# A decoder layer on one core: values, keys and queries of the prologue, and six small pieces of work in the stages, at other places

## The chip, the cores and the metric

The kernel runs on one core of one Trainium2 chip. The metric is the time of one execution on the device in microseconds (us), as the median of several executions. The core's engines are TensorE (PE, matrix multiplication), VectorE (DVE), ScalarE (ACT), GpSimd (POOL) and SyncE (SP); each runs its own instructions strictly in order, and semaphores order them among each other. SP issues most transfers, ACT a few.

## What is computed

Four batches of 512 tokens with 256 features pass through three sublayers, each followed by x + sublayer(x) and a layer norm: gated linear attention, cross attention to a context, and a feed-forward part with a token shift. Shortened:

```python
def _gla_scan(q, k, v, log_gate):            # 16 heads, DK = 8, DV = 16
    def step(state, inp):
        qq, kk, vv, gg = inp
        state = state * gg[..., None] + kk[..., :, None] * vv[..., None, :]
        return state, jnp.einsum('bhd,bhde->bhe', qq, state)
o = _gla_scan(q, k, v, log_sigmoid(x @ Wg1 @ Wg2) / 16)
o = (o - mean(o)) * rsqrt(var(o) + EPS)       # within a head
x = layernorm(x + silu(x @ Wg + bg) * o @ Wo)

Q, K, V = x @ W_q, ctx @ W_k, ctx @ W_v       # 16 heads of 16
attn = softmax(einsum('bqhd,bkhd->bhqk', Q, K) / 4)
x = layernorm(x + einsum('bhqk,bkhd->bqhd', attn, V) @ W_o + b_o)

xr, xk = mu_r * x + (1 - mu_r) * x_prev, mu_k * x + (1 - mu_k) * x_prev
x = layernorm(x + sigmoid(xr @ W_r.T) * (square(relu(xk @ W_k.T)) @ W_v.T))
```

## The kernel before

**Stages.** After a prologue come six stages (`STEPS`). In stage s batch s+2 (called r) is projected and scanned, batch s+1 (o) ends the gated attention and makes keys and queries, batch s (b) runs the cross attention, batch s-1 (f) the feed-forward part and batch s-2 (e) its last norm. A stage is 16 rows n of 4 quarters i; at each (n, i) every engine's code does one score tile of b and whatever tables and `if at == ...` lines put there. So the order of work on every engine is written by hand. A score tile `s{n}.{i}` is a matmul of keys and queries on PE into bank 5 or 6 (L718), then an exponential on ACT (L1230); a row of four tiles is followed by the product with the values on PE (`value_row`, L732). The exponential needs the row maximum of the head: a matmul of queries and keys (L709, L853 in the prologue) and a maximum on DVE (L1652), then `max_parts`, a transpose on PE and a small transfer (`max_rows`) into three extra rows of QS. `Q` and `K` are split in three bfloat16 parts (hi, mid, lo): ACT and DVE take turns on the bank (`first_part`, `rest_of`, `second_part`, `last_part`), SP writes the parts to memory (`part_out`) and reads them back by groups of four heads into KS and QS (`keys_of`, `queries_of`).

**Scans.** The gated attention is 16 scans on DVE (L1797 in the prologue, L1556 later). Each needs a product with the keys on POOL (L2029, L1971), and is followed by a product with the queries on POOL (L1982). Four such products are summed on PE (`reduce_four`, L689), four times a batch; `SUM_QUARTERS` gives the quarters.

**Prologue.** It does the gated attention of batch 0, most of that of batch 1 (`EARLY_SCANS` scans ahead of the first maxima, the rest behind them), the keys and queries of batch 0, the first 16 maxima (heads 0 to 3) and the values of batch 0 (`first_values`, L842: eight matmuls, one behind each of the first eight maxima). `keep_busy` (L957) runs bfloat16 matmuls whose result nobody reads; they only keep PE occupied. `PROLOGUE` lists which bank each matrix uses, in order. SP's queue in the prologue is written out: all K parts of half 0, a transfer of tokens, all K parts of half 1, keys of groups 0 and 1, Q parts, queries of groups 0 and 1.

**Other pieces that the change touches.** `heads_together` issues four small transfers which bring a group's normalised context into the layout of the output projection (`OD`); they wait for `normal`. `invert` is ACT's inverse of the softmax denominators (two instructions, L1260, L1262), which waits for DVE's `spread` (L1672); `normalise` is the product behind it. `group_ends` gives both their quarters. `norm(1, ...)` applies the second layer norm in four DVE instructions (L1542), the `Relu` of the feed-forward part is one ACT instruction for each half (L1201).

## Time and profile before

| | |
|---|---|
| median of 3 executions | 496.71 us (496.16 to 502.71) |
| the profiled execution | 498.83 us, of which 496.5 us are the span that the trace covers |
| busy over the span | PE 438.0 us, DVE 380.2, ACT 286.9, POOL 227.6 |

By stage, from the trace by stretches (a stage is taken from its first score tile):

| stretch | length | PE | DVE | ACT | POOL | granted clock |
|---|---|---|---|---|---|---|
| prologue 0:94.6 | 94.6 | 85.3 | 77.2 | 35.1 | 66.0 | 0.98 |
| stage 0 94.6:190.8 | 96.2 | 84.6 | 74.8 | 59.2 | 59.4 | 0.96 |
| stage 1 190.8:298.2 | 107.4 | 97.9 | 86.9 | 71.9 | 64.4 | 1.00 |
| stage 2 298.2:384 | 85.8 | 78.5 | 70.3 | 57.0 | 29.1 | 1.00 |
| stage 3 384:463 | 79.0 | 67.4 | 52.6 | 49.6 | 8.7 | 0.98 |
| tail 463:496.5 | 33.5 | 24.4 | 18.4 | 14.1 | 0.0 | 0.96 |

How to read it: the rows below are of the timeline unless said otherwise. A row is start, duration, engine, line, what is written from what, the number of instructions; in brackets the idle time of the engine before it and what ended that.
### The profile page before, as it was taken

The numbers are of one execution on the slowest core, as the hardware profiler recorded it, in microseconds if no ns is written. First come the engines' busy times: TensorE is split into PE (matmuls) and PEld (weight loads), VectorE is DVE, ScalarE is ACT, GpSimd is POOL, SyncE is SP. The second block draws the span as 40 slices with busy tenths as digits, with TensorE's granted clock in tenths as the row PEclk, the third lists the DMA queues.
The fourth block names the chain that finished last, engine by engine and source line by source line (L and its number), as shares of the span: only waits on it lengthen the run. The fifth ranks groups of instructions, "written<-read, shape, count | busy, mean of one in ns | idle before, by whom it ended". The sixth has DMA issues, their size and how long they took to land.

```text
span 496.5 us, 6244 instructions
## 1 busy us (share of the span) xinstructions
PE 438.0 (88%) x1919; PEld 185.7 (37%) x1919; DVE 380.2 (77%) x638; ACT 286.9 (58%) x513; POOL 227.6 (46%) x226
## 2 busy tenths in 40 slices
PE   8999888988988899899889888997999888888994
PEld 3433434233432214254343323443433332333563
DVE  4889897967668898577897898599858579754285
ACT  4244362354476666654777866646786545687443
POOL 5568798442158995531489785525022011020000
PEclk9999998999989989999999999999999989999998
DMA  6746565232297521324955304230243310000101
GB/s 202 269 130 178 140 179 133 64 90 73 86 239 184 140 67 46 84 64 120 236 143 131 74 2 116 69 82 2 65 107 75 76 53 3 2 0 1 44 1 44
DMA packets 26512, 47.33 MB, mean 95 GB/s; under 512 B 5456, under 2 KB 16368, under 8 KB 26480
## 3 DMA queue, kind: packets, MB, share of 16 engines
q1 hardware_dynamic: 24512, 44.05, 33.5%
q10 hardware_dynamic: 1968, 2.88, 2.2%
q8 instruction: 16, 0.26, 0.2%
q14 instruction: 16, 0.13, 0.1%
HBM read 35.19 MB, written 9.96 MB: 91 GB/s over the span
## 4 chain that ended last, share of the span: by engine, by line
PE 52%; DVE 27%; ACT 7%; issue 5%; POOL 4%; DMA 2%; SPq 1%; ACTq 1%; DVEq 0%; POOLq 0%
PE bank L657 16%; DVE MX L1652 12%; PE bank L671 9%; PE bank L732 7%; PE bank L718 5%; PE bank L709 5%; DVE W L1556 4%; PE bank L822 3%; ACT PT L1230 3%; POOL W L1982 2%; PE bank L689 2%; DVE st L1529 1%; DMA xT<-in_xT 1%; PE bank L948 1%; DVE den L1672 1%
## 5 line engine op out<-in xcount | busy, mean ns | idle before, releaser
L1652 DVE TENSOR_REDUCE MX<-bank 128x1 f32<-128x512 f32 x256 | 166.1, 680 | 71.6 <-PE bank L709 67.5
L1230 ACT ACTIVATE PT<-bank 128x512 f32<-128x512 f32 x256 | 144.9, 597 | 86.6 <-PE bank L718 81.6
L709 PE MATMUL bank<-KS,QS 96*128 96x512 bf16 x240 | 88.4, 386 | 21.9 <-DVE MX L1652 21.2
L718 PE MATMUL bank<-QS,KS 99*128 99x512 bf16 x256 | 95.9, 388 | 11.2 <-ACT PT L1230 8.5
L732 PE MATMUL bank<-PT,Vs 128*32 128x512 f32 x512 | 70.8, 625 | 4.5 <-ACT PT L1230 4.3
L1982 POOL TENSOR_TENSOR W<-qT,W 128x512 f32<-128x512 f32 x48 | 63.2, 1320 | 20.6 <-DVE W L1556 9.0
L718 PEld LDWEIGHTS bank<-QS,KS 99*128 99x128 bf16 x256 | 24.2, 98 | 101.1 <-issue 58.1
L709 PEld LDWEIGHTS bank<-KS,QS 96*128 96x128 bf16 x240 | 23.4, 98 | 68.9 <-DVE MX L1652 45.2
L1971 POOL TENSOR_TENSOR W<-kT,W 128x512 f32<-128x512 f32 x32 | 41.6, 1299 | 6.7 <-ACT kT L1080 6.7
L1556 DVE TENSOR_TENSOR_SCAN W<-bank,W 128x512 f32<-128x512 f32 x32 | 38.7, 1210 | 0.2 <-ACT bank L1095 0.2
L1797 DVE TENSOR_TENSOR_SCAN W<-bank,W 128x512 f32<-128x512 f32 x32 | 38.1, 1210 | 0.4 <-DVE oS L1816 0.2
L2016 POOL TENSOR_TENSOR MP<-MX,zero 128x16 bf16<-128x16 f32 x15 | 3.6, 241 | 57.4 <-DVE MX L1652 28.9
L1982 POOL TENSOR_TENSOR W<-xr,W 128x512 f32<-128x512 f32 x16 | 21.2, 1332 | 11.4 <-DVE W L1797 11.4
L1949 POOL TENSOR_TENSOR rs<-mv,eps 128x4 f32<-128x4 f32 x9 | 1.8, 202 | 49.5 <-DVE mv L1535 49.5
L732 PEld LDWEIGHTS bank<-PT,Vs 128*32 128x32 f32 x512 | 10.3, 109 | 28.1 <-issue 24.1
L1955 POOL TENSOR_TENSOR OT<-OT,den 128x512 f32<-128x512 f32 x9 | 12.2, 1360 | 17.7 <-ACT den L1262 17.7
L2029 POOL TENSOR_TENSOR W<-xr,W 128x512 f32<-128x512 f32 x16 | 20.2, 1274 | 0.1
L689 PE MATMUL bank<-W,hsel 128*32 128x512 f32 x128 | 17.0, 605 | 2.9 <-POOL W L1982 2.9
L1962 POOL TENSOR_TENSOR ka<-ka 128x512 f32<-128x512 f32 x4 | 4.2, 1040 | 30.8 <-ACT ka L1201 30.8
L957 PE MATMUL bank<-identb 128*128 128x512 bf16 x71 | 17.8, 379 | 0.0
L671 PE MATMUL bank<-wo,oS 128*128 128x256 f32 x64 | 15.1, 380 | 1.8 <-DVE oS L1821 1.8
L657 PE MATMUL bank<-x1T,xwq 128*128 128x512 f32 x32 | 15.0, 596 | 0.9 <-ACT x1T L1330 0.8
(228 smaller groups left out, 721.9 us busy)
## 6 DMA issues: line engine op xcount, KB each, us to landing
W<-v_rows SPq DMA_DIRECT2D x20, 512.0 KB, 8.9
k_parts<-parts SPq DMA_DIRECT2D x24, 128.0 KB, 2.3
KS<-k_parts SPq DMA_DIRECT2D x16, 192.0 KB, 3.5
q_parts<-parts SPq DMA_DIRECT2D x24, 128.0 KB, 2.4
QS<-q_parts SPq DMA_DIRECT2D x16, 192.0 KB, 3.5
cT<-in_cT SPq DMA_DIRECT2D x4, 512.0 KB, 4.3
xtok<-in_x SPq DMA_DIRECT2D x4, 512.0 KB, 10.0
W<-v_rows ACTq DMA_DIRECT2D x4, 512.0 KB, 5.9
```

Of the source, the lines that this page charges most:

```text
L657: ins = pe.matmul(out, w_of(k), x_of(k), start=(k == 0), stop=(k == ND - 1))
L671: ins = pe.matmul(bank(name, b)[:, half * D:(half + 1) * D], x[:, k, tt * P:(tt + 1) * P], w[:, k, :], start=(k == 0), stop=(k == tiles - 1))
L689: ins = pe.matmul(bank(f"o{g}", a)[32 * j:32 * j + 32, :], hsel[:, i, :], W[:, 4 * q + j, :], start=(i == 0), stop=(i == 1))
L709: pe.matmul(bank(n, b)[:, :], QS[0:NS, h, i * P:(i + 1) * P], KS[0:NS, h, :], start=True, stop=True).then_inc(filled(n, b), 1)
L718: pe.matmul(bank(name, b)[:, :], KS[0:NR, h, kt * P:(kt + 1) * P], QS[0:NR, h, :], start=True, stop=True).then_inc(filled(name, b), 1)
L732: ins = pe.matmul(bank(f"pv{g}")[32 * j:32 * j + 32, :], Vs[:, kt, 4 * g + j, :], PT[:, n % 2, j, :], start=(kt == 0), stop=(kt == NT - 1))
L1230: act.activation(PT[:, n % 2, j, :], bank(name, b)[:, :], ACT.Exp).then_inc(emptied(name, b), 1)
L1556: dve.tensor_tensor_scan(W[:, e, :], bank("decay", r)[:, :], W[:, e, :], 0.0, ALU.mult, ALU.add).then_inc(s_done, 1)
L1652: dve.tensor_reduce(MX[:, NT * h + i:NT * h + i + 1], bank(n, b)[:, :], AX.X, ALU.max).then_inc(emptied(n, b), 1)
L1797: dve.tensor_tensor_scan(W[:, e, :], bank("decay", r)[:, :], W[:, e, :], 0.0, ALU.mult, ALU.add).then_inc(s_done, 1)
L1971: pool.tensor_tensor(W[:, e, :], kT[:, :], W[:, e, :], ALU.mult).then_inc(u_pool, 1)
L1982: pool.tensor_tensor(W[:, e, :], qT1 if r == 1 else qT[:, :], W[:, e, :], ALU.mult).then_inc(p_done, 1)
```

## The change

In the prologue:
- PE: the eight value matmuls leave the maxima. Four stand behind K1 (bank 4), where 12 fillers become 5; four behind the first sum of batch 1 (bank 1), where 8 fillers become 6. One filler stands behind each of the first eight maxima instead.
- DVE: scan 1 of batch 1 moves from ahead of the norm (`scale_half`) to behind the first rest of K; the third part of K1 moves ahead of scan 5; scan 7 ahead of the rest of Q0; `EARLY_SCANS` is 12, so scan 12 moves behind the maxima. The bfloat16 copy of the identity moves to ACT.
- SP: keys of group 0 are read as soon as K's half 0 is out, the last two parts of half 1 follow, and the keys of group 1 come behind the queries of group 0. The tokens of batch 1 are loaded at the end.
- ACT: the copy of the batch 1 queries (`qT1`) moves behind the sigmoids, the squares and the decay; each half of the values is copied when it is there.

In the stages:
- the second sum at quarter 49 for 48, the first half's copy (`oS`) at (13, 0) for (12, 2); the last sum of batch 1 one quarter later, with its copy at (1, 1) for (1, 0);
- `heads_together(b, 2)` leaves the end of the stage and stands ahead of that of group 3 in the next stage, behind keys, queries and context;
- in stage 3 the inverse of group 3 at (1, 1) for (1, 0) and its product at (1, 2) for (1, 1);
- the second norm in two halves, at (4, 1) and (4, 2);
- in stage 3 both Relu on DVE instead of ACT.

```diff
-SUM_QUARTERS = {(40, 48, 57, 66)[q]: q for q in range(RQ)}
+SUM_QUARTERS = {(40, 49, 57, 66)[q]: q for q in range(RQ)}
-EARLY_SCANS = 13
+EARLY_SCANS = 12
+FIRST_BUT_ONE = ((0, 1), (0, 2))
-    ends = [(1, f, NG - 1, FIRST_THING)] if f is not None else []
+    ends = [(1, f, NG - 1, FIRST_BUT_ONE if f == LAST - 1 else FIRST_THING)] if f is not None else []
...
 # SP, a stage
+                    heads_together(f, 2)
                     heads_together(f, 3)
...
-                if b is not None and b < LAST:
-                    heads_together(b, 2)
...
 # PE
-                late = NT * (H + at[0]) + at[1] - (o == 1)
+                late = NT * (H + at[0]) + at[1] - 2 * (o == 1)
...
                 by_feature("K1", 0, xwk, 1, cT)
-                keep_busy("gt0", 0, 12)
+                for n in range(NT):
+                    first_values(n)
+                keep_busy("gt0", 0, 5)
...
                 reduce_four(1, 0)
-                keep_busy("s0.0", 0, 8)
+                for n in range(NT, 2 * NT):
+                    first_values(n)
+                keep_busy("s0.0", 0, 6)
                 for h in range(4):
                     for i in range(NT):
                         first_max(h, i)
-                        if h < 2:
-                            first_values(NT * h + i)
-                        else:
-                            keep_busy("s0.0", 0, 1)
+                        keep_busy("s0.0", 0, 1)
...
 # ACT
-                if at == (12, 2):
+                if at == (13, 0):
                     act.wait_ge(r_done, count(RQ, r, RQ // 2))
...
-                if at == (1, 0):
+                if at == ((1, 1) if o == 1 else (1, 0)):
                     act.wait_ge(r_done, count(RQ, o, RQ))
...
-                if at in ((9, 1), (10, 1)):
+                if at in ((9, 1), (10, 1)) and f < LAST - 1:
...
 # DVE
-                if at == (4, 1):
+                if at in ((4, 1), (4, 2)):
                     dve.wait_ge(*full_of("t1", f - 1))
                     dve.wait_ge(x3_done, count(NT, f, 0))
-                    norm(1, xb, x2, x2_done, f)
+                    norm(1, xb, x2, x2_done, f, ((0, 1), (2, 3))[at[1] - 1])
...
+                if at in ((9, 1), (10, 1)) and f == LAST - 1:
+                    m = at[0] - 9
+                    z = bank(f"f{m}")[:, :]
+                    dve.wait_ge(*full_of(f"f{m}", f))
+                    dve.wait_ge(*full_of("w1", f - 1))
+                    dve.scalar_tensor_tensor(ka[:, m, :], z, 0.0, zero[:, 0:1].broadcast_to([P, S]), ALU.max, ALU.max).then_inc(emptied(f"f{m}"), 1)
```

**DVE in the prologue, from the gate of batch 0 to the parts of the queries.** `oS` is the output of the gated attention, `W` the scans, `xtok` the residual, `parts` the bfloat16 parts. Before:

```order
L1816 TENSOR_TENSOR oS<-bank,kz 128x512
L1797 SCALAR_TENSOR_TENSOR W<-bank,W 128x512
L1821 TENSOR_TENSOR oS<-bank,oS 128x512 x2
L1510 SCALAR_TENSOR_TENSOR bank<-bank,parts 128x512
L1797 SCALAR_TENSOR_TENSOR W<-bank,W 128x512
L1826 TENSOR_TENSOR xtok<-bank,xtok 128x512
L1529 BN_STATS st<-xtok 128x6 x2
L1826 TENSOR_TENSOR xtok<-bank,xtok 128x512
L1529 BN_STATS st<-xtok 128x6 x2
L1535 BN_AGGR mv<-st 128x2 x4
L1514 TENSOR_TENSOR parts<-bank,parts 128x512
```

Of the change:

```order
L1827 TENSOR_TENSOR oS<-bank,kz 128x512
L1832 TENSOR_TENSOR oS<-bank,oS 128x512 x2
L1517 SCALAR_TENSOR_TENSOR bank<-bank,parts 128x512
L1808 SCALAR_TENSOR_TENSOR W<-bank,W 128x512 x2
L1837 TENSOR_TENSOR xtok<-bank,xtok 128x512
L1536 BN_STATS st<-xtok 128x6 x2
L1837 TENSOR_TENSOR xtok<-bank,xtok 128x512
L1536 BN_STATS st<-xtok 128x6 x2
L1542 BN_AGGR mv<-st 128x2 x4
L1521 TENSOR_TENSOR parts<-bank,parts 128x512
```

The scan between the two products that write `oS` is gone, so the norm (the pair that writes `oS` from a bank and itself) stands directly behind the gate, and two scans stand ahead of the residual.

**SP's queue in the prologue, from the K parts to the queries.** `KS` and `QS` are the keys and queries that PE reads. Before:

```order
L475 DMA k_parts<-parts 16x8x512 x3
L550 DMA xtok<-in_x 128x4x256
L475 DMA k_parts<-parts 16x8x512 x3
L464 DMA KS<-k_parts 48x1x2048
L464 DMA KS<-k_parts 32x1x2048
L464 DMA KS<-k_parts 16x2048
L464 DMA KS<-k_parts 48x1x2048
L464 DMA KS<-k_parts 32x1x2048
L464 DMA KS<-k_parts 16x2048
L475 DMA q_parts<-parts 16x8x512 x3
L469 DMA QS<-q_parts 48x1x2048
```

Of the change:

```order
L475 DMA k_parts<-parts 16x8x512 x4
L464 DMA KS<-k_parts 48x1x2048
L464 DMA KS<-k_parts 32x1x2048
L464 DMA KS<-k_parts 16x2048
L475 DMA k_parts<-parts 16x8x512 x2
L475 DMA q_parts<-parts 16x8x512 x3
L469 DMA QS<-q_parts 48x1x2048
L469 DMA QS<-q_parts 32x1x2048
L469 DMA QS<-q_parts 16x2048
```

The tokens and the second set of keys no longer stand ahead of the Q parts; four K parts instead of six are ahead of the first keys.

**PE in the prologue, from K1 to the first maxima.** Before:

```order
L657 MATMUL bank<-cT,xwk 128x512 x2
L957 MATMUL bank<-identb 128x512 x12
L679 MATMUL bank<-ident,x1b 128x128 x8
L657 MATMUL bank<-x1T,xwq 128x512 x4
L657 MATMUL bank<-ka,wg 128x512 x4
L689 MATMUL bank<-W,hsel 32x512 x4
L957 MATMUL bank<-identb 128x512 x8
L853 MATMUL bank<-KS,QS 128x512
L842 MATMUL bank<-xwv,cT 128x256
L853 MATMUL bank<-KS,QS 128x512
```

Of the change:

```order
L658 MATMUL bank<-cT,xwk 128x512 x2
L843 MATMUL bank<-xwv,cT 128x256 x4
L959 MATMUL bank<-identb 128x512 x5
L680 MATMUL bank<-ident,x1b 128x128 x8
L658 MATMUL bank<-x1T,xwq 128x512 x4
L658 MATMUL bank<-ka,wg 128x512 x4
L690 MATMUL bank<-W,hsel 32x512 x4
L843 MATMUL bank<-xwv,cT 128x256 x4
L959 MATMUL bank<-identb 128x512 x6
L854 MATMUL bank<-KS,QS 128x512
L959 MATMUL bank<-identb 128x512
```

The value matmuls (`xwv,cT`) stand ahead of the transposes and ahead of the maxima; between the maxima stand fillers.

## Rows read from the trace of the kernel before

**Rows 1.** PE's waits, 94:497: engine, line, releaser, total us, times, longest.
```profile
PE bank L709 <- DVE MX L1652: 21.2, 36, 1.5
...
PE bank L718 <- DMA cT<-in_cT: 1.5, 1, 1.5
```

**Rows 2.** Timeline: start, us, engine, line, out<-in, count, idle before; gate and norm.
```profile
47.26 1.08 ACT L1365 ACTIVATE bank<-bank 128x512 f32<-128x512 f32 x2
...
53.08 1.26 DVE L1821 TENSOR_TENSOR oS<-bank,oS 128x512 f32<-128x512 f32 x2
...
54.40 3.72 PE L671 MATMUL bank<-wo,oS 128*128 128x256 f32 x16 [1.79 <-DVE oS L1821]
```

**Rows 3.** Timeline, 59 to 69 us: statistics to the query projection.
```profile
59.67 0.38 DVE L1535 BATCH_NORM_AGGREGATE mv<-st 128x2 f32<-128x6 f32 x4
...
59.68 2.75 PE L957 MATMUL bank<-identb 128*128 128x512 bf16 x12
...
60.37 0.29 ACT L1420 ACTIVATE rs<-mv,eps 128x4 f32<-128x4 f32 x1
...
63.25 1.09 PE L679 MATMUL bank<-ident,x1b 128*128 128x128 f32 x8 [0.82 <-ACT x1b L1425]
65.13 3.67 PE L657 MATMUL bank<-x1T,xwq 128*128 128x512 f32 x8 [0.79 <-ACT x1T L1330]
```

**Rows 4.** Timeline, 67 to 78 us: query parts, their transfers, first maximum.
```profile
67.83 0.70 DVE L1510 SCALAR_TENSOR_TENSOR bank<-bank,parts 128x512 f32<-128x512 f32 x1 [1.07 <-ACT parts L1039]
...
69.57 0.67 DVE L1514 TENSOR_TENSOR parts<-bank,parts 128x512 bf16<-128x512 f32 x1
...
70.05 1.84 SPq L475 DMA_DIRECT2D q_parts<-parts  x3
...
72.83 3.69 SPq L469 DMA_DIRECT2D QS<-q_parts  x6
...
77.31 0.59 PE L853 MATMUL bank<-KS,QS 96*128 96x512 bf16 x1 [2.24 <-issue]
```

**Rows 5.** PE by stretches: bounds, length, busy, count, granted clock, DMA share, GB/s.
```profile
77.00:80.70 3.70, 3.39 (x9) 0.54 0.67 153
...
179.60:183.00 3.40, 3.40 (x13) 0.51 0.00 0
```

**Rows 6.** Timeline, 85 to 101 us: last maxima, scans, first score tiles.
```profile
85.61 4.87 DVE L1652 TENSOR_REDUCE MX<-bank 128x1 f32<-128x512 f32 x8 [1.06 <-PE bank L853]
...
91.32 3.44 DVE L1797 TENSOR_TENSOR_SCAN W<-bank,W 128x512 f32<-128x512 f32 x3
...
92.61 4.70 POOL L1982 TENSOR_TENSOR W<-xr,W 128x512 f32<-128x512 f32 x3 [8.20 <-DVE W L1797]
...
94.61 0.39 PE L718 MATMUL bank<-QS,KS 99*128 99x512 bf16 x1 [0.17 <-DMA QS<-mrow]
...
94.91 1.28 DVE L1782 SCALAR_TENSOR_TENSOR ab<-kz,ab 128x1024 f32<-128x1024 f32 x1
...
97.37 1.06 PE L689 MATMUL bank<-W,hsel 128*32 128x512 f32 x8 [0.80 <-POOL W L1982]
...
98.79 3.08 DVE L1652 TENSOR_REDUCE MX<-bank 128x1 f32<-128x512 f32 x5 [0.81 <-PE bank L709]
```

**Rows 7.** Timeline, stage 0, quarter 48: the second sum.
```profile
173.21 1.06 PE L689 MATMUL bank<-W,hsel 128*32 128x512 f32 x8 [1.36 <-POOL W L1982]
```

**Rows 8.** Stage 1, quarter 7: a piece of the chain, then a timeline row.
```profile
198.81 4.09 DMA cT<-in_cT
...
202.88 0.10 PEld L718 LDWEIGHTS bank<-QS,KS 99*128 99x128 bf16 x1 [1.99 <-ACT PT L1230]
```

**Rows 9.** Timeline, stage 3: a score tile behind the inverse; the second Relu.
```profile
398.36 0.39 PE L718 MATMUL bank<-QS,KS 99*128 99x512 bf16 x1 [1.78 <-ACT PT L1230]
...
443.24 0.60 ACT L1201 ACTIVATE ka<-bank 128x512 f32<-128x512 f32 x1
```

**Rows 10.** Chain of work in order of time, stage 3: start, us, what.
```profile
399.23 1.89 DVE MX L1652 x3
```

More of the change, by code:

```diff
@@ L540, in prologue @@
                 sp.wait_ge(ks_set, 3)
-                for m, done in ((0, K_out0), (1, [K_out] * 3)):
-                    sp.wait_ge(K_hi0, m + 1)
-                    part_out("k_parts", 0, 0, m, done[0])
-                    sp.wait_ge(K_mid0, m + 1)
-                    part_out("k_parts", 0, 1, m, done[1])
-                    sp.wait_ge(*read(f"K{m}", 0))
-                    part_out("k_parts", 0, 2, m, done[2])
-                    if m == 0:
-                        sp.wait_ge(x1_0, NT)
-                        sp.dma_start(xtok[:, :, :], xtok_v[1]).then_inc(xt_in, 16)
+                sp.wait_ge(K_hi0, 1)
+                part_out("k_parts", 0, 0, 0, K_out0[0])
+                sp.wait_ge(K_mid0, 1)
+                part_out("k_parts", 0, 1, 0, K_out0[1])
+                sp.wait_ge(K_hi0, 2)
+                part_out("k_parts", 0, 0, 1, K_out)
+                sp.wait_ge(*read("K0", 0))
+                part_out("k_parts", 0, 2, 0, K_out0[2])
                 for p in range(3):
                     sp.wait_ge(K_out0[p], 16)
-                for g in range(2):
-                    for key_slots in SLOTS_K:
-                        keys_of(0, g, *key_slots)
+                for key_slots in SLOTS_K:
+                    keys_of(0, 0, *key_slots)
+                sp.wait_ge(K_mid0, 2)
+                part_out("k_parts", 0, 1, 1, K_out)
+                sp.wait_ge(*read("K1", 0))
+                part_out("k_parts", 0, 2, 1, K_out)
                 sp.wait_ge(Q_hi0, 1)
@@ L561, in prologue @@
                 part_out("q_parts", 0, 2, 0, Q_out0[2])
-                sp.wait_ge(Q_out0[0], 16)
-                queries_of(0, 0, *SLOTS_Q[0])
-                sp.wait_ge(Q_out0[1], 16)
-                queries_of(0, 0, *SLOTS_Q[1])
-                sp.wait_ge(Q_out0[2], 16)
-                queries_of(0, 0, *SLOTS_Q[2])
+                for p in range(3):
+                    sp.wait_ge(Q_out0[p], 16)
+                    queries_of(0, 0, *SLOTS_Q[p])
+                for key_slots in SLOTS_K:
+                    keys_of(0, 1, *key_slots)
                 for query_slots in SLOTS_Q:
@@ L1214, in max_rows, with value_half @@
                 act.dma_start(QS[NS:NR, 4 * g:4 * g + 4, :], mrow[:, :]).then_inc(m_in, 16)
+            def value_half(b, m):
+                act.wait_ge(*full_of(f"V{m}", b))
+                if b:
+                    act.wait_ge(pv_done, count(H, b, 0))
+                act.activation(Vs[:, 2 * m:2 * m + 2, :, 0:HD],
+                               bank(f"V{m}", b)[:, :].rearrange("p (t h e) -> p t h e", t=2, e=HD),
+                               ACT.Copy).then_inc(emptied(f"V{m}", b), 1)
             def values_set(b):
                 for m in range(2):
[L1218 to L1223 removed]
+                    value_half(b, m)
             def exp_tile(b, n, j):
@@ L1388, in prologue @@
                 act.sem_inc(v_half, 1)
+                act.activation(identb[:, :], ident[:, :], ACT.Copy).then_inc(idb, 1)
                 for m in range(ND):
@@ L1863, in prologue @@
                 rest_of("K", K_hi0, 0, 1.0, K_rest0)
+                first_scan(1, 1)
                 first_scan(1, 2)
```

21 lines of the change are left out of this document (7 added, 14 removed), and 4 rows, old and new, of the table PROLOGUE.

## The prediction

> **What bounds the kernel now.** I read the busy shares by stage first, then PE's waits, then the timeline where the change acts. In the stages PE is the fullest engine, and what it waits for longest is DVE's maxima: 21.2 us in 36 pieces [rows 1]. There is no single bound. A saving counts only where the wait that it removes ends last. In the prologue one can follow such a chain by eye: gate and norm of batch 0, the output projection, statistics, transposes, query projection, query parts, their way through memory into QS, and only then the first maximum, ahead of which PE stands idle for 2.24 us [rows 4]. Behind the maxima come the first score tile and all stages. So a microsecond taken from that chain moves everything behind it, unless DVE or POOL, which carry the scans, become late.
>
> **Prologue, up to the queries.** Two things leave the path ahead of the norm. ACT's copy of the batch 1 queries went ahead of the sigmoids [rows 2]; a copy of that shape is 0.60 us long [rows 9] and starts of neighbours lie 0.5 apart, so 0.5. The scan between gate and norm costs 3.44/3 = 1.15 [rows 6]. The norm goes from 53.08 to about 51.4, PE's projection from 54.40 to 52.8. On DVE the scan comes back at once: two stand ahead of the residual now, so the statistics gain only the 0.5. To this come about 0.2 where DVE waited for PE's result (my estimate, PE being 1.6 earlier), and 0.3 because ACT did the first part of K1 from 60.05, when the statistics end (59.67 + 0.38), to 60.37 [rows 3]; K1 is done 1.6 earlier now. Sum 1.0: transposes at 62.3 for 63.25, query projection at 64.1 for 65.13.
>
> PE's fillers hide nothing there but idle time: 12 take 2.75 us, 0.23 each [rows 3]; four value matmuls (half as long as K1's, about 0.43 each) and five fillers take 2.9. As PE begins 1.6 earlier but the transposes only 1.0, its gap ahead of them grows from 0.82 to about 1.2. ACT's copy of half the values fits into the 0.79 and more for which it would wait for the query projection.
>
> DVE waited 1.07 us ahead of the rest of Q0 at 67.83 [rows 4]. It now has one scan more in front of it (1.15) and comes 1.0 earlier, so it is there at 66.76 - 1.0 + 1.15, and with some slack in my sum I put the rest at 67.1. The last part of Q0 had a scan ahead of it and has none: it waits only for ACT's second part (0.60), at 67.1 + 0.70 + 0.60 + 0.05 = 68.45 for 69.57.
>
> **SP.** Its queue was the second reason: the first Q transfer was issued at 70.05, after all K parts and two sets of keys, though its data were there at about 67.8. Each issue takes 1.84/3 = 0.61. Now the third Q part goes out when it is made, 68.45 + 0.67 = 69.15. A part needs 70.05 to 72.83 = 2.8 until it may be read, so the third read is issued at 71.9; before it was at 72.83 + 2 x 0.61 = 74.05, and the first maximum 3.26 later. The first maximum comes at 75.2 for 77.31: **2.1 us**. The work put behind (keys of group 1, tokens, context) is needed first in stage 0, some 20 us later. If DVE is later than I say, bound 1.0; if both reads and transfers are faster because keys and 512 KB of tokens are gone from the queues, 2.8.
>
> **The first maxima.** Before, the first eight were interleaved with value matmuls, and PE ran at a granted 0.54 over 77.0 to 80.7, that is at 1.2 GHz, after the idle time [rows 5]. From 77.31 to DVE's ninth at 85.61 are 8.30 us. Without them DVE sets the pace: 4.87/8 = 0.61 each. After the first matmul (0.4) eight take 4.9, and the sum on PE (1.06) leaves DVE a gap of about 0.8. That is 6.1: the ninth at 81.3 for 85.61. The gain has become 4.3, the first score tile is at 90.4 for 94.61. PE is ready for 75.2: query and gate projections, the sum, four value matmuls (1.7) and six fillers (1.4) end there. Bounds: 2.0 (PE still slow) to 2.6 for this step.
>
> **Behind the maxima.** One scan more: DVE reaches stage 0's first maximum at 96.19 - 4.3 + 1.15 = 93.05. POOL has four products for three; three took 4.70 [rows 6], so four take 6.3 from the end of the first scan, 88.3, to 94.6. PE's last sum then starts at 94.6 for 97.37. Queued behind it are PE's sixth maximum and everything after. The sixth is made at 96.0; DVE has four maxima ready and makes the fifth meanwhile, until 93.05 + 5 x 0.62 = 96.15. So its pause of 0.81 ahead of 98.79 disappears, and the fourth maximum is at 94.9: **3.9 us** for the prologue. Each microsecond by which POOL ends after 95 costs one.
>
> **The stages.** Second sum, stage 0: PE waited 1.36 for POOL [rows 7]. A score tile and a maximum now go ahead of it, whose work (starts 0.22 apart) is done in that time: 0.5. Bounds: a loss of 0.3, if ACT's copy (0.60) at (13, 0) makes a score tile late, and 1.36.
>
> Group 2's transfers: the page of waits shows PE waiting 1.5 us for the context in stage 1 [rows 1], and that load leaves SP behind these four transfers. It will be some 2.5 earlier. But the weight load of the same score tile, at the same 202.88, is released by ACT's exponential after 1.99 us; the context lands at 198.81 + 4.09 = 202.90 [rows 8]. Both end together, ACT's queue stays, so 0 (bounds 0 and 1.5). In stages 2 and 3 PE has no such wait.
>
> Inverse in stage 3: a score tile waits 1.78 for ACT, which stands in the inverse [rows 9]. But DVE's maxima follow one another into 401.12 and are what the chain runs through [rows 10]; the product of the inverse only changes places among them. 0 (bounds 0 and 1.78). Relu: ACT's second stands in a stretch in which it has no pause, 0.5 for 0.60, the first does not. On DVE such an instruction takes 0.70 [rows 4] where DVE waits for PE. Bounds 0 and 1.2. The second norm in halves adds no work and PE's next turn of x2 has over 3 us of slack: 0. The identity copy, the late sum of batch 1 (above) and the tokens' load: 0.
>
> **Sum:** 3.9 + 0.5 + 0.5 = 4.9 us. The profiled execution takes 498.83, of which 496.5 are its span; by the sum 493.9. The median of the runs shown is 2.1 below it, 496.71, and gives 491.8.
>
> **Rivals.**
> *A, as forecast:* 491.8, with the step bounds about 489.5 to 494.
> *B, one or two new stretches at the lower clock.* Each of those seen lasts 3.4 to 3.7 us at 0.51 to 0.54 [rows 5] and costs up to 3.7 x 0.46 = 1.7 us. For it: the gap ahead of the transposes grows to 1.2, followed by 0.6 of matmul and another 0.8 to 1.0 of idle time, and the query projection behind it is on the path. Against: PE kept 2.4 GHz over 1.79 us of idle ahead of 54.40 [rows 2]. 493.5 to 495.2. The Trainium skill (TensorE: Matmul & The Clock Gate, What's actually happening) says that the gate follows how busy PE has recently been, so that activity releases the throttle; the trace agrees at 77 us, and by that rule moving work out of a gap can cost more than the work.
> *C, the waits named are the true ones.* Context 1.5 and inverse 1.78 count in full besides: 488.5. For it stand the page's releasers, against it the rows at the same instants.
> *D, the prologue's gain is taken back.* If POOL's products end at 98.3, four us later than I put it, the last sum holds PE as before, and 3.9 are gone: 495.7.
> *E, slower.* Three more stretches at 1.2 GHz in stages, whose gaps shift against before: 4.9 - 3 x 1.7 gives 496.9. It decides from the third stretch on; before there are stretches in stage 0 as well, so that they can also disappear.
>
> **Numbers.** A 0.55, B 0.22, C 0.10, D 0.07, E 0.06. Predicted is A, 491.8. The range 488.0 to 496.0 holds A to D. Faster by over 2% would be under 486.8: every upper bound at once, 0.05. Slower by over 2%, above 506.6: 0.03. Within 2%, about what a measurement of this kernel can tell from no change: 0.92.
>
> **What would show it.** Right: transposes near 62.3, first maximum near 75.2 at full clock, ninth near 81.3, first score tile near 90.4, DVE without a pause in its first six maxima of stage 0, the second sum of stage 0 with almost no wait; the score tile of stage 1's quarter 7 still waiting near 2 us for ACT. Wrong: half clock in the query projection; PE waiting over 1 us more for POOL ahead of the last sum; stage 1 shorter by 1.5.

## The result and the profile after

The changed kernel takes 496.74 us in the median of 22 executions (492.98 to 499.36), the kernel before 498.61 in 22 (496.16 to 502.87): a ratio of 0.9944 with a 95% interval of 0.9919 to 0.9969. The ratio goes by the means (496.23 and 499.03), not by the medians, which lie only 1.9 us apart. It says 2.8 us faster (1.5 to 4.0), within 2%. I had forecast 491.8, from 4.9 us off a median of 496.71. That median, of three executions, lay 1.9 below the one of 22, so the miss of 4.9 us in the absolute time has two parts: the base, and a gain that was put too high. The profiled execution of the changed kernel takes 498.95 us, its span is 497.0.

PE's waits from 94 us on, the same view as [rows 1] (engine, line, releaser, total us, times, longest):

```profile
PE bank L710 <- DVE MX L1665: 25.2, 36, 1.5
...
PE bank L690 <- POOL W L1993: 0.4, 2, 0.2
```

POOL's 1.36 of [rows 7] and the wait for the context, 1.5 in [rows 1], have gone from the list. PE waits 4.0 us more for DVE's maxima (25.2 for 21.2).

The prologue in the timeline of the changed kernel (rows as in [rows 2] to [rows 6]):

```profile
52.76 1.29 DVE L1832 TENSOR_TENSOR oS<-bank,oS 128x512 f32<-128x512 f32 x2
...
61.10 1.24 PE L959 MATMUL bank<-identb 128*128 128x512 bf16 x5
...
63.23 1.09 PE L680 MATMUL bank<-ident,x1b 128*128 128x128 f32 x8 [0.88 <-ACT x1b L1431]
65.11 5.37 PE L658 MATMUL bank<-x1T,xwq 128*128 128x512 f32 x8 [0.79 <-ACT x1T L1335]
...
77.96 0.38 PE L854 MATMUL bank<-KS,QS 96*128 96x512 bf16 x1
...
93.12 0.39 PE L719 MATMUL bank<-QS,KS 99*128 99x512 bf16 x1
...
96.00 4.26 DVE L1665 TENSOR_REDUCE MX<-bank 128x1 f32<-128x512 f32 x7
```

The gap ahead of the transposes is 0.88 us, where I had expected 1.2. The query projection is 5.37 us long and not 3.67 [rows 3]. PE by stretches shows why (columns as in [rows 5]; the second has all engines' columns in the order PE, PEld, DVE, ACT, POOL):

```profile
65.20:68.80 3.60, 3.60 (x5) 0.53 0.49 139
...
7.00:11.00 4.00, 3.77 (x5) 1.65 (x6) 1.20 (x5) 1.22 (x3) 4.00 (x1) 0.57 0.83 204
```

That is rival B: the projection behind the gap runs at a granted 0.53, half of 2.4 GHz. There is a second new stretch at 7 us. The norm then stands at 52.76, as in e11, which has the same stretch (52.77); in the seven other executions of the new order it stands at 51.13 to 51.72. So the whole prologue was 1.0 to 1.6 us late before its changed part began, and the profiled execution shows the first score tile only 1.5 us earlier (93.12 for 94.61 in [rows 6]) and DVE's first maximum of stage 0 hardly earlier at all (96.00 for 96.11).

The two traces must not be subtracted as they stand. I read 17 profiled executions, and in most the stretches at half clock lie at other places. Some of them agree: e5 and e10, one program, have all four near the same times, and the changed kernel and e9, one program too, differ only by the stretch at 7 us and the 1.4 us by which all is later. But e11 and e15, again one program, have none in common but one near 400 us and the one at the end. Every execution also comes with its mean granted clock, and the time follows it. A fit of time = kernel's own constant + slope x clock over all executions of all kernels here has a slope of 3.6 us for 0.01 of mean clock, and leaves 0.9 us of scatter (the kernel before alone scatters by 1.9, one standard deviation, and 71% of that variance goes with the clock). By it the difference between the kernels at equal clock is 3.75 us; the changed kernel's mean clock is 0.9798 and that of the kernel before 0.9819, which gives 0.8 back. The fit is a correlation: a stretch costs more or less by where it lies, so two kernels whose stretches lie at different places can be off in it by more than its error. How far is said at the end of the account.

### The profile page after: what moved, and what is told of

The parts are those of the page before. It is cut to its first block, busy times and chain, and to the rows that moved or that the text cites. A ratio compares the mean times of both kernels' runs of the same rounds, so it can differ in the third digit from the quotient of the medians.

```text
span 497.0 us, 6253 instructions
## 1 busy us (share of the span) xinstructions
PE 441.1 (89%) x1918; PEld 186.3 (37%) x1918; DVE 378.0 (76%) x639; ACT 286.1 (58%) x512; POOL 227.7 (46%) x226
## 4 chain that ended last, share of the span: by engine, by line
PE 56%; DVE 25%; ACT 8%; issue 6%; POOL 2%; ACTq 1%; DMA 0%; DVEq 0%; POOLq 0%
PE bank L658 16%; DVE MX L1665 11%; PE bank L672 10%; PE bank L733 8%; PE bank L719 6%; PE bank L710 6%; ACT PT L1235 3%; PE bank L823 3%; PE bank L690 2%; DVE W L1563 2%; DVE W L1808 1%; DVE st L1536 1%; DVE den L1685 1%; PE bank L950 1%; POOL W L1993 1%
## 5 line engine op out<-in xcount | busy, mean ns | idle before, releaser
L710 PE MATMUL bank<-KS,QS 96*128 96x512 bf16 x240 | 88.6, 387 | 26.5 <-DVE MX L1665 25.2
L1993 POOL TENSOR_TENSOR W<-qT,W 128x512 f32<-128x512 f32 x48 | 62.2, 1300 | 23.6 <-DVE W L1563 10.7
L1982 POOL TENSOR_TENSOR W<-kT,W 128x512 f32<-128x512 f32 x32 | 42.6, 1331 | 6.7 <-ACT kT L1082 6.7
L1993 POOL TENSOR_TENSOR W<-xr,W 128x512 f32<-128x512 f32 x16 | 21.2, 1331 | 9.8 <-DVE W L1808 9.8
L959 PE MATMUL bank<-identb 128*128 128x512 bf16 x70 | 18.9, 379 | 0.0
L658 PE MATMUL bank<-x1T,xwq 128*128 128x512 f32 x32 | 16.7, 655 | 0.9 <-ACT x1T L1335 0.8
```

Source lines behind the costliest of these rows:

```text
L658: ins = pe.matmul(out, w_of(k), x_of(k), start=(k == 0), stop=(k == ND - 1))
L710: pe.matmul(bank(n, b)[:, :], QS[0:NS, h, i * P:(i + 1) * P], KS[0:NS, h, :], start=True, stop=True).then_inc(filled(n, b), 1)
L1982: pool.tensor_tensor(W[:, e, :], kT[:, :], W[:, e, :], ALU.mult).then_inc(u_pool, 1)
L1993: pool.tensor_tensor(W[:, e, :], qT1 if r == 1 else qT[:, :], W[:, e, :], ALU.mult).then_inc(p_done, 1)
```

## The experiments

"At 0.981" is the time that the fit gives at that mean clock, with twice its standard error. Each ratio is taken against the executions of the kernel before beside that run, and is not the quotient of the medians (for e1 that would be 1.0014). The row of the kernel before pools its executions beside the 15 runs; its ratio is 1 by definition.

| kernel | runs | median us | ratio, 95% interval | mean clock | at 0.981 |
|---|---|---|---|---|---|
| before | 111 | 499.47 | 1 | 0.9819 | 499.55 ± 0.2 |
| changed | 22 | 496.74 | 0.9944 (0.9919 to 0.9969) | 0.9798 | 495.8 ± 0.4 |
| e9 changed again | 12 | 497.16 | 0.9936 (0.9907 to 0.9965) | 0.9792 | 495.7 ± 0.5 |
| e1 prologue | 12 | 499.25 | 0.9981 (0.9947 to 1.0014) | 0.9806 | 498.2 ± 0.5 |
| e2 stages | 12 | 500.94 | 1.0018 (0.9988 to 1.0048) | 0.9767 | 498.8 ± 0.5 |
| e3 9 fillers | 12 | 495.20 | 0.9942 (0.9912 to 0.9972) | 0.9798 | 495.3 ± 0.5 |
| e4 13 scans | 10 | 495.82 | 0.9926 (0.9891 to 0.9962) | 0.9809 | 495.0 ± 0.6 |
| e6 queue | 8 | 495.79 | 0.9942 (0.9903 to 0.9982) | 0.9852 | 498.2 ± 0.6 |
| e7 values | 8 | 497.66 | 0.9965 (0.9929 to 1.0002) | 0.9841 | 499.1 ± 0.6 |
| e8 gate | 8 | 497.02 | 0.9954 (0.9911 to 0.9997) | 0.9850 | 498.5 ± 0.6 |
| e12 halves alone | 12 | 500.33 | 1.0020 (0.9983 to 1.0056) | 0.9796 | 499.1 ± 0.5 |
| e13 sums alone | 12 | 499.25 | 1.0017 (0.9991 to 1.0043) | 0.9787 | 498.6 ± 0.5 |
| e14 inverse, Relu | 12 | 498.80 | 0.9989 (0.9962 to 1.0016) | 0.9835 | 499.7 ± 0.5 |
| e11 norm whole | 6 | 493.46 | 0.9873 (0.9826 to 0.9920) | 0.9858 | 495.9 ± 0.7 |
| e15 norm whole again | 9 | 495.21 | 0.9914 (0.9879 to 0.9948) | 0.9849 | 496.1 ± 0.6 |
| e5 combined | 6 | 492.83 | 0.9871 (0.9812 to 0.9930) | 0.9860 | 495.2 ± 0.7 |
| e10 combined again | 6 | 492.76 | 0.9861 (0.9825 to 0.9898) | 0.9867 | 494.7 ± 0.7 |

### Prologue or stages: e1, e2

e1 is the kernel before with the diff's edits of the prologue, e2 with those of the stages.

> Only the edits of the prologue, on the kernel before; the eight edits of the stages are left off. The changed kernel gained 0.56%, 2.8 us, over 22 runs of each. Theory 1 (the prologue carries the whole gain; in an execution without new half-clock stretches it is about 4, with one, in the query projection, about 2): 0.990 to 0.996 of the kernel before, and in its trace the first score tile near 93 and the value row of stage 0 near 99.2 (before 101.05). Theory 2 (the extra scan and the POOL product behind the maxima give the prologue back, and the stages carry the gain): 0.998 to 1.002. The trace should also tell whether the query projection runs at half clock again, as it did at 65.3 to 68.6 in the changed kernel.

> Only the edits of the stages (second sum, heads and context, inverse, halves of the norm, Relu), on the kernel before; the prologue is as it was. Theory 1: 0.999 to 1.002, since each stage of the changed kernel was 0.45 to 0.7 us longer than before in the profiled execution, so they gain nothing and may lose up to 2 us. Theory 2: 0.993 to 0.996, they carry the gain. My prediction's sum gave them 1.0 us (0.998).

Neither is told from no change by its runs. e2 fell in theory 1's range, e1 in theory 2's, so neither theory stands whole. At equal clock the prologue alone gave 1.4 and the stages alone 0.8, together 1.6 less than the 3.75 of both, which is more than the errors of the fit (some 0.9 together); why is open. What these two gave is in the traces. e1's projection ran at full clock (3.67 us long), and its first score tile came at 90.21; then a stretch at half clock from 95.2 to 102 put the value row of stage 0, the first matmul with the values, at 98.55. e2's execution had no half clock in its first 98 us: it shows the old prologue at full clock, and its first score tile stood at 92.56, not at 94.61 [rows 6].

These two traces also show what one of the edits of the stages does, the last sum of batch 1 one quarter later. DVE's first maxima of stage 0 in e12, with the old order throughout this part, and in e2, with the old prologue and the later sum:

```profile
94.04 1.87 DVE L1652 TENSOR_REDUCE MX<-bank 128x1 f32<-128x512 f32 x3
96.72 3.08 DVE L1652 TENSOR_REDUCE MX<-bank 128x1 f32<-128x512 f32 x5 [0.81 <-PE bank L709]
```

```profile
94.06 4.86 DVE L1658 TENSOR_REDUCE MX<-bank 128x1 f32<-128x512 f32 x8
```

DVE's pause ahead of its fourth maximum [rows 6] stands in all seven executions with the sum at its old place (before, e1, e6, e7, e8, e12, e14) and in none of the ten with the later sum. Both executions reach the norm at 52.71, but the value row comes at 98.98 in e12 and at 98.11 in e2. So this edit gives 0.9 us even with the old prologue, and it is missing in e1.

### Fillers and scans: e3, e4

```diff
-                keep_busy("gt0", 0, 5)      # e3
+                keep_busy("gt0", 0, 9)
-EARLY_SCANS = 12                            # e4
+EARLY_SCANS = 13
```

> The changed kernel with 9 fillers in place of 5 ahead of the transposes of the residual's norm, four of 0.22 us, as long as TensorE stood idle there (0.88 us). If the half clock in the query projection (5.37 us long in place of 3.67) comes from the thinner work ahead of it, it runs at full clock now and the kernel is faster than the changed one by up to 1.7 us (about 0.990 to 0.992 of the kernel before). If that stretch is set by something else (chance, or the fillers that run at any rate), the projection is at half clock in this trace too, or the ratio stays at 0.993 to 0.996.

> The changed kernel with 13 scans ahead of the maxima, as before, so that 3 and not 4 run behind them (one of 1.14 us) and the POOL product that waits for the last of them starts earlier; VectorE's first maximum has no slack lost by it if the scans ahead still end before the first maximum of TensorE (77.96). Theory 1 (scans ahead of the maxima were late; moving one behind them is free): the ratio is 0.993 to 0.998, no better than the changed kernel, first maximum of VectorE up to 1.1 us later than 78.38. Theory 2 (the scan and the POOL product behind the maxima took back the prologue's gain): VectorE's stage 0 maxima start near 95 in place of 96.00, the value row of stage 0 near 98.2, and the ratio is 0.990 to 0.992.

e3: the projection ran at full clock, but the ratio is that of the changed kernel. Timeline of e3, the gap ahead of the transposes closed:

```profile
59.69 1.89 PE L959 MATMUL bank<-identb 128*128 128x512 bf16 x8
61.60 1.09 PE L680 MATMUL bank<-ident,x1b 128*128 128x128 f32 x8
```

Of six executions with 5 fillers and the new order, three had the stretch in the projection (the profiled one, e9 and e11, near 65 us); of three with 9 fillers (e3, e5, e10) none. The other three, e1, e4 and e15, have the same gap of 0.89 and run at full clock, so the gap alone doesn't decide it, and the counts are too small to call the filler the cause. Where both run at full clock the four fillers change nothing: from the norm to the value row it is 44.79 us in e3 and 44.78 in e15.

e4: POOL has three products behind the maxima again and not four. The value row of stage 0 comes at 95.23 with 5 fillers, against 96.30 in e15 with the scan behind the maxima; with 9 fillers it comes at 95.43 and 95.38 (e5, e10), against 95.92 in e3. Part of these differences lies ahead of the change, since the norm stands at 51.13 in e3 and at 51.72 in e5. From the norm to the value row it is 43.71 to 43.80 us with 13 scans ahead of the maxima (e4, e5, e10) and 44.78 and 44.79 with 12 (e15, e3). DVE starts stage 0 at 91.98 in e4 and at 93.06 in e15. So the extra scan behind the maxima costs 1.0, the size that theory 2 had; the ratio, 0.9926, lies between the ranges of both. DVE's first maximum lost nothing (75.45 against 75.45 in e15).

### The parts of the prologue: e6, e7, e8

> The kernel before with the new order of SyncE's transfers in the prologue alone (queries ahead of the second group of keys, token transfer last). Read at full clock, from executions without a half-clock stretch in the first 95 us: the kernel with old prologue had TensorE's first maximum at 76.83 and the first score tile at 92.78, the one with the whole new prologue at 74.64 to 74.95 and 90.17 to 90.56; of those 2 us the norm ahead already gave 1.1 (query projection 64.76 to 63.48..63.80). My prediction's step 3 left the queue 1.0 to 1.1 of its 2.1: first maximum 1.0 us earlier than 76.83 with the projection at its old place, near 75.8, and the first score tile near 91.8. Rival: the transfer of the queries is not what the maxima wait for, the first maximum stays within 0.2 of 76.8.

> The kernel before with the value projection alone moved from among the first eight maxima to the fillers' places ahead of the transposes and ahead of the maxima. My prediction's step 4 gave to this, together with the full clock there, 2.2 us of its 4.3. Theory now: nearly all of those were the half-clock stretch at 77.15 to 80.7 in the execution shown, which other executions of the same prologue don't have; so against the full-clock times of the old prologue (first maximum 76.83, first score tile 92.78) the distance between the two, 15.95 us, shrinks by 0.3 to 0.5 only. If my step was right it shrinks by 1.5 or more.

> The kernel before with VectorE's and ScalarE's own moves of the prologue alone: copy of the identity to ScalarE, the query's copy behind the squares, one scan behind the norm of the gate, last part of K1 ahead of a scan, 13 scans ahead of the maxima as before. My step 1: norm of the gate from 52.71 to 51.1 to 51.5 (measured so far with the whole prologue: 51.13 to 51.45), query projection 64.76 to 63.7, and the first maximum 76.83 to 75.8, first score tile 92.78 to 91.8 or later since the scan moved still lies ahead of the maxima. Rival: the first maximum stays at 76.8 since the transfers bound it.

All three had full clock up to 98 us. The old prologue at full clock (e2, e12) has the first maximum at 76.83 and 76.81, and PE's first maximum of stage 0, behind the first score tile, at 92.78 and 92.60. The expectations took 92.78 for the first score tile; here PE's first maximum of stage 0 is compared.

| | norm | query projection | first maximum PE | same, DVE | first of stage 0 |
|---|---|---|---|---|---|
| old, e12 | 52.71 | 64.75 | 76.81 | 77.22 | 92.60 |
| queue, e6 | 52.85 | 64.90 | 75.33 | 76.71 | 92.08 |
| values, e7 | 52.70 | 64.75 | 77.60 | 78.02 | 92.93 |
| gate, e8 | 51.35 | 63.70 | 75.12 | 75.53 | 91.27 |
| whole, e15 | 51.52 | 63.88 | 75.03 | 75.45 | 90.56 |

The queue alone brings PE's first maximum 1.5 us forward but the stage only 0.5: DVE, still in its scans, takes the first tile 1.4 us after it is there. I had expected 75.8 and 91.8, and they came at 75.33 and 92.08. The gate alone moves the maximum 1.7 and the stage 1.3, to 75.12 and 91.27, both further than the 75.8 and 91.8 expected. Values alone delay the first maximum by 0.8 and shorten the distance from it to the stage from 15.79 to 15.33. That is 0.5 against e12 and 0.6 against e2 (15.95), about the 0.3 to 0.5 expected and not the 1.5 or more by my step on the first maxima. The three parts add up to 1.5 at this place and the whole gives 2.0; no run says which of them need each other.

### The norm in halves: e9, e11, e12, e15

```diff
-                if at in ((4, 1), (4, 2)):
+                if at == (4, 1):
-                    norm(1, xb, x2, x2_done, f, ((0, 1), (2, 3))[at[1] - 1])
+                    norm(1, xb, x2, x2_done, f)
```

This is e11 and e15, on the changed kernel; e12 is its reverse on the kernel before.

> The changed kernel itself, beside the kernel before and the two below on one chip. Over 22 runs it was 0.9944 of the kernel before. Theory now (at full clock the prologue gives 2.2 us, the sums of stage 0 about 0.8, Relu 0.4, what lies around the span 0.3, and the norm's halves cost 0.6 in stage 2, so 3.1 in all): 0.992 to 0.9955. In an execution without a half-clock stretch in the first 99 us the first score tile stands near 90.4 and the value row of stage 0 near 96.2, not at 93.12 and 99.24 as in the profiled one.

> The changed kernel with the norm of the stages in one piece, nothing else. The halves' price by the traces: stage 2 was 88.13 to 88.29 in four executions with the norm in one piece and 88.68 to 88.89 in two with halves, all at full clock. So stage 2 is 88.1 to 88.3 here, TensorE's wait for the maximum at its offset 37 is 1.00 and not 1.37, and the kernel is 0.3 to 0.7 us faster than the changed kernel beside it, which is less than the runs can tell. My prediction had the halves at 0: stage 2 would be 88.7 to 88.9 here.

> The kernel before with the norm of the stages in halves, nothing else. Theory 1 (the halves cost 0.5 to 0.6 us in stage 2 and nothing elsewhere): 1.000 to 1.002, stage 2 at 88.7 to 88.9 at full clock where the kernel before has 88.18, mean granted clock over the runs as that of the kernel before (0.981 to 0.983). Theory 2 (they also make half-clock stretches more frequent: five sets of runs with halves had a mean granted clock of 0.977 to 0.981, five sets without, outside the kernel before, 0.984 to 0.987, and e11 was 2.2 us faster on average than e9 beside it): mean granted clock below 0.980, and 1.003 to 1.006.

> The changed kernel with the norm of the stages in one piece once more (e11 had six runs, 0.9873 with an interval of 0.9%; the changed kernel 0.9936 beside it). Theory 1 (halves cost 0.5 to 0.6): 0.991 to 0.994. Theory 2 (halves cost the clock too, 2 us or more): 0.986 to 0.990, with a mean granted clock of 0.984 or more.

DVE in stage 2, timelines of e15 (whole) and then e12 (halves):

```profile
325.01 1.37 DVE L1549 TENSOR_SCALAR x<-x1b,mv,rs 128x256 f32<-128x256 f32 x4
326.30 1.28 DVE L1665 TENSOR_REDUCE MX<-bank 128x1 f32<-128x512 f32 x2
```

```profile
329.62 0.72 DVE L1542 TENSOR_SCALAR x<-x1b,mv,rs 128x256 f32<-128x256 f32 x2
330.63 1.29 DVE L1652 TENSOR_REDUCE MX<-bank 128x1 f32<-128x512 f32 x2 [0.29 <-PE bank L709]
331.84 0.73 DVE L1542 TENSOR_SCALAR x<-x1b,mv,rs 128x256 f32<-128x256 f32 x2
```

With halves DVE reaches the next maximum before PE has filled the bank and waits 0.29. The second half then stands between maxima that are ready. PE pays at offset 37.7 from the start of stage 2 (e12, then the stage by stretches):

```profile
335.07 0.39 PE L709 MATMUL bank<-KS,QS 96*128 96x512 bf16 x1 [1.37 <-DVE MX L1652]
```

```profile
335.00:338.50 3.50, 3.43 (x14) 0.56 0.00 0
297.33:386.88 89.55, 82.61 (x392) 0.98 0.28 73
```

The stage at full clock is 88.68, 88.75 and 88.89 with halves (changed, e9, e4). Without, it is 88.13 to 88.33 in ten executions and 88.53 in the eleventh (e10). The wait at this place is 1.00 in the kernel before. So the fixed price is 0.5, of which 0.37 arise at this wait. There may be a second one by the clock: the stretch at 335 stood in three of six executions with halves (e2, e3, e12) and in none of eleven without; a stage with it takes 89.55 to 89.71. Over the runs, the changed kernel (34) has a mean clock of 0.980 and the same without halves (15) 0.985, and it is 1.8 us slower on average; at equal clock the two do not differ beyond the fit's error. e11 was 3.1 us faster than e9 beside it (0.9873 and 0.9936) where 0.3 to 0.7 was expected, with stage 2 at 88.23 and the wait at 0.99 as expected. e12 came out between its theories (clock 0.9796, ratio 1.002 with an interval holding both, so about 1 us slower), e15 between its own too. But e13, which has no halves, has a mean clock of 0.9787, as low as the kernels with them, so a low clock is no mark of the halves alone. The traces show the fixed price. That the halves cost 1 to 2 us in all, the rest of it by the clock, is what both pairs of runs point to and is not shown.

### Sums, inverse, Relu: e13, e14

> The kernel before with the second sum of stage 0 and the copies that go with it at their new places, nothing else. My prediction: 0.5 us. By the traces: in stage 0 TensorE's wait of 1.36 us for GpSimd's product is gone and its wait for the maximum at offset 82.4 stands at 81.7, so 0.7 us at full clock; stage 0 at 89.2 to 89.4 with one half-clock stretch (89.94 to 90.11 before). Ratio 0.997 to 1.000. Rival: a second half-clock stretch, which in the old order falls on TensorE's wait and costs nothing (90.02 with 7.2 us at half clock), costs 1.4 in the new (90.65 to 90.70 with 7.3), so nothing is left: 0.999 to 1.002.

> The kernel before with the inverse at stage 3's start one place later and the two Relu of stage 3 on VectorE, nothing else. The inverse: TensorE's wait of 1.78 us for ScalarE at offset 11.6 of stage 3 goes and one of 1.37 for VectorE's maximum comes at 11.4; both orders stand level again at offset 14.4, so 0. Relu: the wait of 1.37 at offset 59.7 becomes 0.89, 0.42 us in all, where my prediction had 0.5. What lies outside the span was 2.3 to 2.4 us in every kernel with the old stages and 2.0 in those with the new ones; if the Relu or the inverse does that, it is 2.0 here. Ratio 0.998 to 1.000.

The second sum: PE's wait for POOL ahead of it is gone in e13 as in the changed kernel, and the last wait of that stretch is the same for both orders, 1.34 us for DVE, but earlier. Changed kernel:

```profile
176.30 0.39 PE L719 MATMUL bank<-QS,KS 99*128 99x512 bf16 x1 [0.82 <-ACT PT L1235]
...
180.93 0.39 PE L710 MATMUL bank<-KS,QS 96*128 96x512 bf16 x1 [1.34 <-DVE MX L1665]
```

It stands at offset 81.69 of stage 0, counted from the value row (180.93 - 99.24); in e6, with the old order, at 82.42. So 0.7 us. As the rival said, it can be lost again: stage 0 with a second stretch at half clock is 90.65 to 90.70 in the new kernels and 90.02 in the kernel before, whose stretch at 179.6 [rows 5] covered that wait. It isn't always lost: e13 and e12 both have 6.8 us at half clock from 114 us on, and there stage 0 takes 90.46 with the new order and 91.15 with the old, so the 0.7 is kept. e13's ratio of 1.0017 lies in the range of the rival, with a low mean clock of 0.9787. At equal clock e13 is 0.9 faster than the kernel before (499.55 - 498.6), and by its trace it should be 1.6: 0.7 here and the 0.9 of the later last sum. So "nothing left" is what the runs show of the time, and not what the traces show of the order.

Inverse and Relu: the changed kernel's rows for [rows 9] are

```profile
397.98 0.39 PE L710 MATMUL bank<-KS,QS 96*128 96x512 bf16 x1 [1.36 <-DVE MX L1665]
...
446.97 1.06 PE L733 MATMUL bank<-PT,Vs 128*32 128x512 f32 x8 [0.89 <-ACT PT L1235]
```

The 1.78 us for ACT became 1.36 for DVE, and at offset 14.4 of stage 3 the orders are level: 0 from the inverse. The second row's wait was 1.37 before. A value row further on stands at offset 71.15 of stage 3 in the kernel before and at 70.69 in e15, and up to that wait the two agree within 0.01, so the Relu gives 0.5. e14's runs show no difference. What lies around the span was 2.3 to 2.4 us on average in the kernel before and in e1, e6, e7, e8 and e13, and 2.0 to 2.2 in all others, of which e12 has only the new norm and e14 only the new inverse and Relu; why is open.

### The combination: e5, e10

> The changed kernel with 9 fillers ahead of the transposes, 13 scans ahead of the maxima, and the norm of the stages in one piece again (four tiles at one place, as before). In the traces so far the halves of the norm cost VectorE 0.37 us in stage 2: its first half ran so early that it then waited 0.28 us for TensorE, and every maximum behind it was 0.37 us later. If that is so, the wait of TensorE at offset 37 of stage 2 is 1.00 again and not 1.37, stage 2 is 88.2 us long and not 88.7 to 88.9 (at full clock), and the kernel is 0.988 to 0.991 of the kernel before, faster than the changed one (0.9944) and than the one with 13 scans (0.9926). If the halves cost nothing outside one execution, it stays at 0.991 to 0.994.

> The combined kernel (9 fillers, 13 scans, norm in one piece) again, since six runs gave 0.9871 with an interval of 1.2%. From the stretches at full clock it should be faster than the changed kernel by 0.7 (value row 95.23 to 95.92 for the scan) and 0.6 (stage 2 at 88.2 for 88.8), so by 1.3 to 1.6 us: 0.989 to 0.9925 of the kernel before. If it stays below 0.989, something else gained too; if it is no faster than the changed kernel, both readings fall.

In both traces the wait in stage 2 is 0.99, as expected; the stage takes 88.21 in e5 and 88.53 in e10. Nine fillers, 13 scans and the norm whole, with all the rest of the change, has the lowest ratio here: 0.9861 (0.9825 to 0.9898), 7 us less than before and some 3.7 less than the changed one; the intervals of e11 and e15, with the norm whole alone, overlap with it. Its gain over the changed kernel was larger than the 1.3 to 1.6 by the stretches at full clock. Its mean clock of 0.987 against 0.979 of e9 beside it accounts for 2.7 of it by the fit.

## Why the prediction was wrong

The steps of the prologue, in us. The two middle columns are full-clock executions of the old prologue and the new one.

| | before, as profiled | old, full clock (e12) | forecast | new, full clock (e15) | changed, as profiled |
|---|---|---|---|---|---|
| norm | 53.08 | 52.71 | 51.4 | 51.52 | 52.76 |
| transposes | 63.25 | 62.88 | 62.3 | 62.00 | 63.23 |
| query projection | 65.13 | 64.75 | 64.1 | 63.88 | 65.11 |
| rest of Q0 | 67.83 | 67.45 | 67.1 | 66.58 | 69.30 |
| last part of Q0 | 69.57 | 69.19 | 68.45 | 67.94 | 70.66 |
| first maximum | 77.31 | 76.81 | 75.2 | 75.03 | 77.96 |
| DVE's ninth | 85.61 | 83.53 | 81.3 | 81.15 | 84.08 |
| first score tile | 94.61 | 92.37 | 90.4 | 90.33 | 93.12 |
| DVE, stage 0 | 96.11 | 94.04 | 93.05 | 93.06 | 96.00 |
| last sum | 97.37 | 95.30 | 94.6 | 94.33 | 97.27 |
| value row, stage 0 | 101.05 | 98.98 | | 96.30 | 99.24 |

(The prediction has 96.19 for the 96.11; that number is in no row, and changes its sum by less than 0.1.)

- **Mechanism of the prologue: right.** Each forecast time is met within 0.6 us, the last five within 0.3, by an execution at full clock. DVE has no pause in its first six maxima of stage 0, as forecast. e15 itself:

```profile
81.15 4.28 DVE L1665 TENSOR_REDUCE MX<-bank 128x1 f32<-128x512 f32 x7 [0.82 <-PE bank L854]
...
90.33 0.39 PE L719 MATMUL bank<-QS,KS 99*128 99x512 bf16 x1 [0.18 <-DMA QS<-mrow]
```

- **The failed term: "The first maxima", "the gain has become 4.3".** I took the granted 0.54 at 77 us [rows 5] for a property of the old order and its end for a gain of the change. From PE's first maximum to DVE's ninth I read 8.30 and forecast 6.1, a gain of 2.2. The 6.1 came (6.12 in e15, and 6.11 in e7 by the value matmuls alone), but the old order at full clock takes 6.7, not 8.30 (e2, e12). So 0.6 of the 2.2 belongs to the change and 1.6 to a stretch at half clock, which stood in three of five executions of the old prologue (before, e13, e14). With it gone the ninth gains 2.4 (83.53 in e12, 81.15 in e15), not 4.3. I also tied the stretch to the idle time ahead of it. PE idles 2.12 us there in e12 and in e13 alike; e12 runs on at full clock and e13 at half, so the trace bears on that less than I said.
- **The prologue as a whole: 3.9 forecast, 2.7 measured** at full clock, by the value row (98.98 in e12, 96.30 in e15). Of the 2.7 the later last sum of batch 1 gives 0.9 (98.11 in e2) and the edits of the prologue 1.8. The forecast had that edit inside its 3.9, as the pause of 0.81 that disappears, and counted it to the prologue; e2 shows the pause gone with the old prologue.
- **Rival B: it came, at its price.** The stretch in the query projection costs 1.7: from the norm to the value row it is 46.48 us in e9 and in the changed kernel, 44.78 in e15. I set it beside the forecast as an alternative, though the new order with 5 fillers has it in half of its executions, about as often as the old order has its own at 77 us. On average the change trades one stretch for another. That is why the 1.6 us of clock in the forecast are not in the result. The Trainium skill (TensorE: Matmul & The Clock Gate, What's actually happening) ties the gate to how busy PE has been; the closed gap of e3 and its full clock agree with it without proving it, and e15, with the gap open and full clock too, shows that more than this gap decides.
- **Behind the maxima: the order and the times right.** D, which needed POOL's products to end at 98.3, is refuted: they end at 97.20 even in the profiled execution, and at 94.27 in e15. The scan moved behind the maxima costs 1.0 (e4). The forecast has it as the 1.15 by which DVE comes later, but doesn't ask whether 13 scans ahead would be better.
- **Second sum: 0.5 forecast, 0.7 at full clock,** which a second stretch takes back in some executions and not in others (e13).
- **Group 2 and context: 0, right; C refuted.** The wait of 1.5 for the context became one of 1.50 for ACT in the same place, offset 11.8 of stage 1. The old order of the transfers has it under either name: the context in the kernel before, e1, e7 and e14, ACT in e6, e8, e12 and e13, each time 1.5 long. So the two do end together:

```profile
201.75 0.39 PE L719 MATMUL bank<-QS,KS 99*128 99x512 bf16 x1 [1.50 <-ACT PT L1235]
```

- **Inverse 0, right; Relu 0.5, right.**
- **Halves of the norm: "adds no work ... 0" failed.** I asked only when PE needs x2. The price was on DVE's side, which set the pace there: 0.5 fixed, and perhaps more by the clock.
- **The sum.** With the measured terms, 2.7 + 0.7 + 0.5 - 0.5, and 0.3 around the span, it is 3.7; the fit says 3.75 at equal clock. The clock takes 0.8 of it, which leaves the 2.8 to 3.0 found. That the two agree so closely is partly luck. For single parts the same terms and the fit lie 0.6 to 1.1 apart: by the terms e12 should be 0.2 slower, and by the fit it is 0.4 faster; e14 should be 0.8 faster and is 0.1 slower; e2 should be 1.9 faster and is 0.8 faster. The other 1.9 us of the miss in the absolute time are the base: three executions could not say where in 494.7 to 503.2 the kernel's median lies. With the same 4.9 taken from 498.61 the forecast would have been 493.7, still 3.0 below the time measured.

## What to carry to other kernels

Before a stretch at half clock is counted as a cost that a change removes, look for it in a second execution; what is left at full clock is the term of the sum, and the clock is a term of its own with a chance. Compare traces by offsets from a common point within a stage: the waits named here repeat there to some 0.02 us between executions with equal stretches ahead of them, while totals scatter by 8. Take a pause apart before it is credited to an edit, since two edits that were made together can look like one. And moving half an instruction group earlier on the engine that sets the pace is not free, even where it adds no work: it can run dry first and be in the way afterwards.

## What the runs showed of the hardware

The same program on one core scattered from 494.7 to 503.2 us over 111 executions, and most of that goes with the clock: each 0.01 of the mean granted clock, some 10 us of TensorE at half of 2.4 GHz, came with 3.6 us. So a stretch at half clock costs about a third of its length on average: 1.7 us of 3.4 in the query projection, nothing where it covers a wait for DVE.

Not all of the scatter is the clock. Stage 1 ran at full clock in 16 of the 17 executions and took 107.03 to 108.31 us. Between e11 and e15, one program, the difference of 1.2 us arises at one place, where PE stands idle in e11 and the profile shows nothing that it waits for:

```profile
268.24 0.38 PE L710 MATMUL bank<-KS,QS 96*128 96x512 bf16 x1 [1.08 <-issue]
```

This idle time is 0.21 in the kernel before, 0.74 in the changed one and none in e15. So the changed kernel's profiled execution lost 0.5 us more here, and no edit of stage 1 is needed for it. The cause is open.

POOL's products between the last maxima and the last sum are of one shape, but the one that runs beside DVE's logarithm of the gate (both operands in SBUF, the on-chip memory) takes 2.25 us, the other three 1.23 each ((5.94 - 2.25) / 3, from the first row); it is 2.24 or 2.25 in all 17 executions. It is always the last product, too, and no run tells the two apart. I had taken the mean of 4.70 / 3 for each.

```profile
91.27 5.94 POOL L1993 TENSOR_TENSOR W<-xr,W 128x512 f32<-128x512 f32 x4 [8.10 <-DVE W L1808]
94.68 1.40 DVE L1793 SCALAR_TENSOR_TENSOR ab<-kz,ab 128x1024 f32<-128x1024 f32 x1
...
94.95 2.25 POOL L1993 TENSOR_TENSOR W<-xr,W 128x512 f32<-128x512 f32 x1
```
